# Five 128-row passes instead of six 96-row passes in two split matrix products of an audio tower

## What is computed

```python
h = token_stage(x)                  # depthwise conv, 192x192, relu, max over pairs -> 375 tokens,
                                    # real part of a 2-D DFT, layer norm
xh = layernorm(h)
w  = xh @ w_qkv                     # 192 -> 768: the FIRST PROJECTION
...                                 # token statistics attention on w, then @ w_out
h  = h + attention
n  = layernorm(h) * g1 + b1         # scores, the 56 lowest tokens get softmax attention,
...                                 # the others a mix with a pooled token
h  = hidden + merged
n2 = layernorm(h) * g2 + b2
ffn = gelu(n2 @ W1 + bf1) @ W2 + bf2     # n2 @ W1, 192 -> 768: the FIRST FEED-FORWARD PRODUCT
return h + ffn
```

## Time and profile before

| what | value |
|---|---|
| median of 3 runs | 632.99 us (630.13 to 634.43) |
| the profiled execution, its own time | 630.36 us |
| its span | 628.5 us |
| mean granted TensorE clock | 0.938 |
| TensorE matmul busy (PE) | 537.3 us, 85% |
| TensorE weight loads busy (PEld) | 441.9 us, 70% |
| VectorE / ScalarE / POOL busy | 71% / 37% / 11% |
| chain of waits, share by engine | PE 58%, DVE 21%, ACT 12%, issue 6% |

### The profile page before, as it was taken

The page is one execution under the profiler, slowest core; times in us unless marked ns, Lnnn a source line. Parts: engine busy times, 40 slices in busy tenths (PEclk is TensorE's granted clock), DMA queues, the critical chain, the costliest instruction groups (busy, mean ns, idle before and its releaser), DMA issues.

```text
span 628.5 us, 9490 instructions
## 1 busy us (share of the span) xinstructions
PE 537.3 (85%) x3344; PEld 441.9 (70%) x3344; DVE 444.2 (71%) x1239; ACT 234.6 (37%) x619; POOL 68.4 (11%) x67
## 2 busy tenths in 40 slices
PE   1637588969998999999999999899989998959896
PEld 1425476848776977787877887687779776847676
DVE  5777577577877887888778887788778573853240
ACT  1124022621465145702581157214651457013611
POOL 0010011002020022002100301030201220020000
PEclk9987598688999999999999999999999999977699
DMA  8421000010001000000001000100000000000001
GB/s 215 143 63 38 0 2 1 1 37 2 1 1 37 18 3 2 21 17 18 0 0 37 18 0 0 37 18 0 0 0 19 1 1 1 2 19 1 1 7 31
DMA packets 8217, 12.73 MB, mean 20 GB/s; under 512 B 1896, under 2 KB 6722, under 8 KB 8189
## 3 DMA queue, kind: packets, MB, share of 16 engines
q1 hardware_dynamic: 8189, 12.37, 7.3%
HBM read 10.07 MB, written 2.30 MB: 20 GB/s over the span
## 4 chain that ended last, share of the span: by engine, by line
PE 58%; DVE 21%; ACT 12%; issue 6%; DMA 1%; POOL 1%; DVEq 0%; ACTq 0%; SPq 0%; POOLq 0%
PE xb L1163 8%; PE yb L1078 7%; PE zb L1078 7%; PE xb L1108 5%; PE yb L1340 5%; ACT probs L967 3%; PE xb L1117 3%; ACT w_sq L892 2%; PE xb L1078 2%; DVE dw L401 2%; DVE nr L557 2%; ACT w_s L891 2%; DVE w_sq L508 2%; PE xb L1144 2%; DVE junk L516 2%
## 5 line engine op out<-in xcount | busy, mean ns | idle before, releaser
L815 POOL TENSOR_TENSOR rs<-ve,half 125x3 f32<-125x3 f32 (+1 forms) x32 | 33.4, 1045 | 529.3 <-DVE ve L366 451.7
L383 DVE SCALAR_TENSOR_TENSOR dw<-x_in,w_dw_sb,dw 96x750 f32<-96x750 f32 x84 | 79.0, 990 | 0.2
L1078 PE MATMUL xb<-xhT,w_qkv_sb 96*128 96x376 f32 x288 | 64.0, 368 | 4.8 <-DVE xhT L468 3.4
L1078 PE MATMUL yb<-n2T,w_sb 96*128 96x376 f32 x288 | 60.2, 350 | 4.2 <-DVE n2T L703 3.2
L1078 PEld LDWEIGHTS xb<-xhT,w_qkv_sb 96*128 96x128 f32 x288 | 52.7, 206 | 11.3 <-DVE xhT L468 6.8
L1163 PE MATMUL xb<-scratch,w_sq 128*125 128x192 f32 x288 | 52.7, 346 | 5.2 <-ACT scratch L903 5.2
L1163 PEld LDWEIGHTS xb<-scratch,w_sq 128*125 128x125 f32 x288 | 51.3, 202 | 5.8 <-DVE scratch L530 5.8
L1078 PEld LDWEIGHTS yb<-n2T,w_sb 96*128 96x128 f32 x288 | 49.1, 191 | 6.9 <-DVE n2T L703 4.2
L1340 PE MATMUL yb<-w_sb,gelu 128*125 128x192 f32 x252 | 48.7, 336 | 5.3 <-ACT probs L967 5.3
L1340 PEld LDWEIGHTS yb<-w_sb,gelu 128*125 128x125 f32 x252 | 40.3, 187 | 10.5 <-ACT probs L967 6.5
L972 ACT ACTIVATE probsT<-zb 125x384 f32<-125x384 f32 x48 | 26.4, 549 | 24.0 <-PE zb L1274 24.0
(11 more groups left out here) (190 smaller groups left out, 1122.1 us busy)
## 6 DMA issues: line engine op xcount, KB each, us to landing
x_in<-in_x SPq DMA_DIRECT2D x8, 567.0 KB, 4.2
out<-res_f SPq DMA_DIRECT2D x7, 281.2 KB
probsT<-in_w_qkv SPq DMA_DIRECT2D x1, 576.0 KB, 7.1
w_out_sb<-in_w_out SPq DMA_DIRECT2D x1, 576.0 KB
w_sb<-in_w SPq DMA_DIRECT2D x1, 576.0 KB
probsT<-in_w SPq DMA_DIRECT2D x1, 576.0 KB, 4.2
rows_sb<-in_rows SPq DMA_DIRECT2D x1, 504.0 KB
dft_n_sb<-in_dft_n SPq DMA_DIRECT2D x1, 493.5 KB
```

Of the source, the lines that this page charges most:

```text
L383: ins = dve.scalar_tensor_tensor(out=dw[0:C, c, :], in0=src, scalar=w_dw[:, c, k:k + 1], in1=dw[0:C, c, :], op0=ALU.mult, op1=ALU.add)
L815: pool.tensor_tensor(out_[:], in_[:], half3[:] if len(in_.shape) == 3 else half3[:, 0, :], ALU.pow).then_inc(rs.sem, 1)
L1078: ins = mm(o, a[:, k], b[:, l], start=start and k + l == 0, stop=stop and k == 1)
```

## The change

Both products now contract 128 rows where they can. The first 128 channels are slot 0 of the weights (high) and slot 2 (low). The last 64 channels stand twice, in rows 0 to 63 and 64 to 127 of slot 1 (high) and slot 3 (low). On the tokens' side slot 0 is the high part of the first 128 channels, slot 2 their low part, and slot 1 has the high part of the last 64 in rows 0 to 63 and their low part in rows 64 to 127, so that one pass gives high x high and high x low for them. The low part of the weights of the last 64 channels is a pass of 64 rows, the third of five.

To get the last 64 channels into both halves of the partitions, the transposes become 3 transposes of 128 channels and 6 ordinary float32 matmuls against the identity, each with 64 columns of tokens as stationary operand, one with its output in partitions 0 to 63 and one in 64 to 127.

```diff
-        w_qkv = sb("w_qkv_sb", [C, 2, CT, IT * 128], fp32r)
+        w_qkv = sb("w_qkv_sb", [128, 4, IT * 128], fp32r)
...
-        n2T = sb("n2T", [C, 2, CT, NE], fp32r)
+        n2T = sb("n2T", [128, 3, NE], fp32r)
...
-        xhT = sb("xhT", [C, 2, CT, NE], fp32r)
+        xhT = sb("xhT", [128, 3, NE], fp32r)
...
-        w_qkv32 = probsT[0:C].rearrange("c j t q -> c (j t q)")[:, 0:CT * IT * 128].rearrange("c (t i) -> c t i", t=CT)
-        w_1_32 = w_qkv32
...
+        w_qkv32 = gelu[:].rearrange("c j n -> c (j n)")[:, 0:2 * IT * 128].rearrange("c (t i) -> c t i", t=2)
+        w_1_32 = w_qkv32
...
-        n2T_ready, n2T_high, n2T_done = signal("n2T_ready"), signal("n2T_high"), signal("n2T_done")
+        n2T_ready, n2T_high, n2T_done = signal("n2T_ready"), signal("n2T_high"), signal("n2T_done", CT)
...
+            def stacked_low(c, parts, bank):
+
+                if c == 0:
+                    return dve.tensor_tensor(parts[:, 2, 0:N], bank[:, 0, 0:N], parts[:, 0, 0:N], ALU.subtract)
+                return dve.tensor_tensor(parts[64:128, 1, 0:N], bank[64:128, 1, 0:N], parts[64:128, 1, 0:N], ALU.subtract)
...
-                    dve.tensor_tensor(xhT[:, 1, c, 0:N], xb[0:C, c, 0:N], xhT[:, 0, c, 0:N], ALU.subtract).then_inc(xhT_done.sem, 1)
+                    stacked_low(c, xhT, xb).then_inc(xhT_done.sem, 1)
...
-                dve.tensor_tensor(n2T[:, 1, :, 0:N], zb[0:C, 0:2, 0:N], n2T[:, 0, :, 0:N], ALU.subtract).then_inc(n2T_done.sem, 1)
+                for c in range(CT):
+                    stacked_low(c, n2T, zb).then_inc(n2T_done.sem, 1)
...
-                    act.activation(xhT[:, 0, c, 0:N], xb[0:C, c, 0:N], ACT.Copy).then_inc(xhT_high.sem, 1)
+                    act.activation(xhT[:, c, 0:N], xb[:, c, 0:N], ACT.Copy).then_inc(xhT_high.sem, 1)
...
-                act.activation(n2T[:, 0, :, 0:N], zb[0:C, 0:2, 0:N], ACT.Copy).then_inc(n2T_high.sem, 1)
+                act.activation(n2T[:, 0:2, 0:N], zb[:, 0:2, 0:N], ACT.Copy).then_inc(n2T_high.sem, 1)
...
+            def stacked_transposes(src, dst):
+
+                for t in range(T):
+                    pe.transpose(dst[0:128, 0, tok(t)], src[:, t, 0:128], ident[0:P, 0:P])
+                for t in range(T):
+                    for r in (0, 64):
+                        ins = mm(dst[r:r + 64, 1, tok(t)], src[:, t, 128:D], ident[0:P, 0:P], start=True, stop=True)
+                return ins
...
+            def stacked_highs(o, w, j, x):
+
+                cols = slice(128 * j, 128 * j + 128)
+                mm(o, w[:, 0, cols], x[:, 0, :], start=True, stop=False)
+                mm(o, w[:, 2, cols], x[:, 0, :], start=False, stop=False)
+                mm(o, w[0:64, 3, cols], x[0:64, 1, :], start=False, stop=False)
+
+            def stacked_lows(o, w, j, x):
+
+                cols = slice(128 * j, 128 * j + 128)
+                mm(o, w[:, 1, cols], x[:, 1, :], start=False, stop=False)
+                return mm(o, w[:, 0, cols], x[:, 2, :], start=False, stop=True)
...
-                transposes(xh, xb).then_inc(xhT_ready.sem, 1)
+                stacked_transposes(xh, xb).then_inc(xhT_ready.sem, 1)
...
-                for c in range(CT):
-                    if j == 0:
-                        pe.wait_ge(*xhT_done.of(b, c + 1))
-                    ins = split_product(xb[:, j % 2, 0:NE], w_qkv[:, :, c, 128 * j:128 * j + 128], xhT[:, :, c, :], c == 0, c == 1)
+                if j == 0:
+                    pe.wait_ge(*xhT_high.of(b))
+                    pe.wait_ge(*xhT_done.of(b, 1))
+                stacked_highs(xb[:, j % 2, 0:NE], w_qkv, j, xhT)
+                if j == 0:
+                    pe.wait_ge(*xhT_done.of(b))
+                ins = stacked_lows(xb[:, j % 2, 0:NE], w_qkv, j, xhT)
...
-                transposes(n2, zb).then_inc(n2T_ready.sem, 1)
+                stacked_transposes(n2, zb).then_inc(n2T_ready.sem, 1)
...
-                for c in range(CT):
-                    ins = split_product(yb[:, j % 2, 0:NE], w_1[:, :, c, 128 * j:128 * j + 128], n2T[:, :, c, :], c == 0, c == 1)
+                stacked_highs(yb[:, j % 2, 0:NE], w_1, j, n2T)
+                ins = stacked_lows(yb[:, j % 2, 0:NE], w_1, j, n2T)
...
+    def stacked(w):
+
+        return np.stack([w[0:128], np.concatenate([w[128:], w[128:]])], 1)
...
-        "w_qkv": tiles(a["L0_attn_w_qkv"], C),
+        "w_qkv": stacked(a["L0_attn_w_qkv"]),
...
-        "w_1": tiles(a["L0_ffn_W1"], C),
+        "w_1": stacked(a["L0_ffn_W1"]),
```

More of the change, by code:

```diff
@@ L72, in audio_tower @@
         slot = sb("slot_sb", [Q, 1])
-        w_1 = sb("w_1_sb", [C, 2, CT, IT * 128], fp32r)
+        w_1 = sb("w_1_sb", [128, 4, IT * 128], fp32r)
         b_1 = sb("b_1_sb", [128, IT])
@@ L264, in split_parts @@
         def split_parts(k):
-            weight, parts = ((w_qkv32, w_qkv), (w_1_32, w_1), (w_k32, w_k), (w_v32, w_v), (w_m[:], w_mp))[k]
+            if k < 2:
+                parts = (w_qkv, w_1)[k]
+                return w_qkv32, parts[:, 0:2, :], parts[:, 2:4, :]
+            weight, parts = ((w_k32, w_k), (w_v32, w_v), (w_m[:], w_mp))[k - 2]
             return weight, parts[:, 0, :, 0:weight.shape[-1]], parts[:, 1, :, 0:weight.shape[-1]]
@@ L802, in _ @@
             pool.memset(half3[:], -0.5).then_inc(consts.sem, 1)
-            for tokens in (xhT, n2T, nT):
-                pool.memset(tokens[:, :, :, N:NE].bitcast(fp32), 0.0).then_inc(pads.sem, 1)
+            for tokens in (xhT, n2T):
+                pool.memset(tokens[:, :, N:NE].bitcast(fp32), 0.0).then_inc(pads.sem, 1)
+            pool.memset(nT[:, :, :, N:NE].bitcast(fp32), 0.0).then_inc(pads.sem, 1)
             pool.memset(w_v[:, :, :, D + 1:DV].bitcast(fp32), 0.0).then_inc(pads.sem, 1)
```

## The result

The changed kernel takes **675.88 us** (675.12 to 677.29, four runs), against 632.75 us for the kernel before (630.13 to 634.43, four runs): the ratio is 1.070, with a 95% interval of 1.0675 to 1.0727. The forecast was 649.5 us, range 638 to 657. The direction was right, the size was not, and the time lies outside the range.

A forecast was written before the change was run, and what follows sets the result against it. The chain of waits was taken as the bound, on TensorE through the feed-forward tiles and transposes, on ScalarE in the loop. Six steps (10.4 us) and the ends (6.3) gave +16.7 on 632.99: forecast 649.5 us, range 638 to 657.

The forecast's parts named there:

- two changes of shape in a tile: Around the 64-row third pass of each tile: two changes at 0.19 us each, 0.38 us added.
- tiles 1 to 5 on the path: In `forward_up`, five tiles at a net 0.21 us each: 1.05 us more per middle step.
- transposes of `xh`: Three transposes and six float32 matmuls instead of six transposes, on the path: +0.48 us, bounds +0.33 and +1.14.
- split of `xhT`: ScalarE and VectorE instructions on more partitions cost no extra time: taken as 0, bounds 0 to 0.1 us.
- split of `n2T`: Two VectorE instructions for one, ahead of L557: taken as 0, at most 0.1 us a step.
- the loop: Six first-projection tiles add 1.26 us to PE, which has 1.13 idle; ScalarE waits 0.2 us, bounds 0 and 0.3.
- PE's idle time before `routed_input`: Sign to look for in the new trace: this idle time down from 1.31 to about 0.5 us.
- drain-only rival: A shape change costs only 0.09 us at the border, the weight load being covered: +5.2 us, 638.2; chance 0.10.
- the one with free changes: Shape changes cost nothing, as 64-row weight loads go in under the running pass: -5.2 us, 627.8; chance 0.10.
- the rival with column groups in turn: Small transpose matmuls' two column groups run one after the other: +5.9 us, 655.6; chance 0.12.
- the rival "Clock": Longer gaps could bring more time at 1.2 GHz; a slice more at half speed costs about 5 us; chance 0.05.
- The ends: First steps, step 8 and the last step, outside the six middle steps: 6.3 us added together.

The follow-up runs named there:

- e3: The changed kernel with the third pass on all 128 rows and six full transposes, so no new change of tile shape: 623.07 us, ratio 0.9881 to before.
- e8: The kernel before with five passes of 96 rows a tile instead of six, one high x low pass left out: 628.84 us, ratio 0.9979.
- e1: The changed kernel with the third pass on all 128 rows, moved behind the second wait, small transpose matmuls kept: 629.31 us, ratio 0.9958 to before.
- e9: e3 with the rank sums using 128 columns of ones instead of 64, one more change of shape removed: 620.48 us, ratio 0.9825 to before.
- e4: The kernel before, six passes a tile, one high x low pass cut from 96 rows to 64: 771.94 us, ratio 1.2214.
- e7: The kernel before plus one 64x64, one-column matmul adding zeros in each tile: 719.40 us profiled, 774.13 to 782.87 us in the other three runs.
- e2: The changed kernel with six full transposes instead of three and six small matmuls, 64-row third pass kept: 673.76 us, ratio 1.064 to before.

## Why the prediction was wrong

Point by point, by its own steps, for one middle step. The measured column comes from laying the two traces on one landmark, the first of L537's instructions in a step (349.33 before, 375.59 in the changed kernel, 1.88 us ahead of the instruction in the earlier trace rows), and taking how much later an instruction starts: L1108 behind VectorE's pooling 0.09 (9.72 after the landmark instead of 9.63), the transposes of `xh` 1.19 (33.57 for 32.38), the matmuls behind them 1.67 (34.83 for 33.16), VectorE's `w_mp` behind the split 1.81 (36.70 for 34.89), the first L1340 behind the loop 2.06 (47.10 for 45.04).

| step of the prediction | forecast | measured |
|---|---|---|
| two changes of shape in a tile | +0.38 | +0.39 |
| tiles 1 to 5 on the path | +1.05 | +1.10 |
| transposes of `xh` | +0.48 | +0.48 |
| split of `xhT` | 0 (bound 0.1) | +0.14 |
| split of `n2T` | 0 (bound 0.1) | +0.09 |
| the loop | +0.2 | +0.25 |
| sum of a step | +1.73 | +2.06 |

**What held.** The reading of the earlier trace rows was right to a hundredth: border and first weight load together, twice in each tile. Only the list of distances to look for had one too many (0.26, 0.27, 0.27, 0.27); the trace has the same 0.39 us in three (0.26, 0.37, 0.27). PE's idle time before `routed_input` came out at 0.48 us, 0.5 forecast. The drain-only rival and the one with free changes are refuted by the tile above, the rival with column groups in turn by L1090. The Trainium skill (page "TensorEngine Tiling (Array Packing)", section "Key Properties") says that a change of tiling mode drains TensorE. The trace agrees with 0.26 instead of 0.17 us at the border; as drain alone the rule would miss half of what the tile pays.

**Two small misses.** The two VectorE instructions of a split, on 128 and on 64 partitions, start 0.58 us apart, where the two on 96 partitions started 0.46 apart (two in 1.00 us, the second 0.54 long):

```profile
383.19 1.00 DVE L468 TENSOR_TENSOR xhT<-xb,xhT 96x375 fp32r<-96x375 f32 x2 [1.68 <-ACT xhT L882]
```

The second of the pair now reads from partition 64 on; whether that or the number of partitions makes the difference no run shows. For `xhT` the delay is on the path. For `n2T` TensorE starts 0.09 us later behind the pooling that follows L557. e3 keeps both (0.14 and 0.11 against e8's trace), which accounts for 0.25 of the 0.27 us between its 66.03 and the 65.76 of e8.

**The step that failed** is the clock. The sum has no term for it; it stands only in the rival "Clock": "a slice more at half speed costs about 5 us", with a chance of 0.05 and half of it outside the range. Its price per slice was near what was seen: at the 0.4 us per us of the third stretch a slice of 16.8 us is an estimated 6.7 us. Wrong was that the number of slices was treated as chance, apart from the change. The prediction found the gaps, 24 new ones in a middle step, and charged their time; it did not ask what TensorE's clock does when its stream has them. The lower level went from 78 to 155 us, 4.6 slices. Of the 26 us between the forecast and the time some 2 are the small misses in six steps, and the other 24 are put to the clock; 77 us at 0.4 would be an estimated 31, so that the price is not the same everywhere. e1, e3 and e9, without the gaps in the tiles, have the clock of before; e4 and e7, with such gaps and without anything else of the change, fall to 0.76 and to 0.83 or less. What stays open is why the changed kernel holds the full clock through five middle steps and e4, with one more pass, in none, and whether a gap without a change of shape would do the same. The runs show that these gaps bring the lower level, not how many of them a kernel bears.

Of the terms of the sum, the six middle steps were sized at 10.4 us. By the full-clock step they would be 12.4; they are 23.4, as the first of them holds 27 us of the lower level. The ends were sized at 6.3 us and are 21.5 (3.95, 5.05 and 12.5 in the first, second and last stretch).

## What to carry to other kernels

A pass over fewer rows is no smaller pass: in a stream of full tiles a matmul of another tile shape costs 0.2 us at each of its two edges here; one edge alone is more than the 0.17 us of the pass that the packing had saved. Fill the rows with what does no harm (here the low x low product, which was already in place), make the transposes ordinary ones, and the same idea gains 1.2% (e3). And whoever adds gaps to TensorE's stream has to price the clock beside them: read the granted clock per stretch, and look at distances between starts, because busy time shows neither.

## What the runs showed of the hardware that was not expected

- A matmul with almost no work in it (64x64, one column), put between two full passes twelve times a step, took the mean granted clock from 0.924 or more to 0.83 and the kernel from 632 to 719 us in its fastest run (e7; the others 774 to 783 us).
- In e4 the clock fell at the end of a stretch in which PE was marked busy for 16.70 of 16.70 us.
- Time at the lower level cost 0.40 us (changed kernel, 11.0 of 27) to 0.43 us (e7, 14.5 of 34) per us in a middle step. Work bound by TensorE alone would lose 0.5; that it is less fits a step that waits for other engines in part, which no run shows apart.
- VectorE reading PSUM at partitions 64 to 127 and writing at 0 to 63 (e2, e3, e9) needs no step in between, so that three ordinary transposes of channels 64 to 191 can serve both halves of a stacked tile.
